# A fused adapter and mixture-of-experts kernel: tile 1 gathered early, gate/up of tile 1 ahead of down of tile 0, gathers four tiles ahead

## The reference

```python
base = jnp.einsum('bsi,oi->bso', x, W_base)
h = jnp.einsum('bsi,ji->bsj', x, Wt)
z = jnp.einsum('bsj,brj->bsr', h, Ab); l = jnp.einsum('bsr,bor->bso', z, Bb)
y = base + jnp.einsum('bso,po->bsp', l, Wp) * sc[:, None, None]
probs = jax.nn.softmax(y @ gate_w.T, axis=-1)
topk_w, topk_idx = jax.lax.top_k(probs, 2)            # then normalised to sum 1
g, u = (jnp.einsum('th,eih->tei', y, w) for w in (w_gate, w_up))
out = x + jnp.einsum('te,teh->th', combine, jnp.einsum('tei,ehi->teh', silu(g) * u, w_down))
```

## Time and profile before

| | |
|---|---|
| median of 3 runs | 370.98 us (370.84 to 372.6) |
| the profiled execution's own time | 370.85 us |
| its span in the trace | 369.0 us |
| PE busy | 351.7 us, 95% of the span |
| ACT, DVE, POOL busy | 179.0, 196.9, 135.3 us |

### The profile page before, as it was taken

How to read it: one execution, slowest core, us unless ns; L and a number is a source line. 1 busy time by engine, 2 the same in 40 slices (tenths; PEclk the granted TensorE clock), 3 DMA queues, 4 the chain that set the end, 5 groups by cost and what they waited for, 6 DMA issues and landing times.

```text
span 369.0 us, 7595 instructions
## 1 busy us (share of the span) xinstructions
PE 351.7 (95%) x2053; PEld 310.5 (84%) x2053; DVE 196.9 (53%) x272; ACT 179.0 (48%) x242; POOL 135.3 (37%) x85
## 2 busy tenths in 40 slices
PE   8999999998889999999999999999999999999980
PEld 4777788777789999999999999999999998898860
DVE  0566799782185445362854727548263556556210
ACT  2488611621464554645647356474555467454320
POOL 0000000024532525382753635546355455532131
PEclk9999999999999999999999999999999999999996
DMA  7994755873759676949297793956948575921322
GB/s 280 399 434 142 293 222 185 265 291 96 260 175 301 171 203 138 297 76 309 46 283 249 189 322 68 285 178 210 314 95 254 116 213 167 304 37 10 51 33 36
DMA packets 28914, 73.78 MB, mean 200 GB/s; under 512 B 3441, under 2 KB 3569, under 8 KB 28785
## 3 DMA queue, kind: packets, MB, share of 16 engines
q1 hardware_dynamic: 19904, 54.30, 41.9%
q0 software_dynamic: 8960, 18.89, 23.5%
HBM read 60.59 MB, written 19.92 MB: 218 GB/s over the span
## 4 chain that ended last, share of the span: by engine, by line
PE 80%; DMA 8%; issue 5%; DVE 2%; ACT 1%; POOL 1%; DVEq 1%; POOLq 1%; SPq 0%; ACTq 0%
PE bank L632 35%; PE bank L651 20%; PE bank L566 4%; PE bank L505 4%; PE bank L610 4%; PE bank L506 3%; PE bank L507 3%; PE bank L402 3%; DMA xg<-y_rows,gidx 3%; DMA w_raw<-wall 2%; DMA head_sb<-head 2%; PE bank L433 1%; DMA y_rows<-y_st 1%; PE bank L515 1%; POOL xg L1111 1%
## 5 line engine op out<-in xcount | busy, mean ns | idle before, releaser
L1128 POOL DMA_INDIRECT out<-ys,sidx x40 | 78.3, 1957 | 132.1 <-ACT ys L780 65.8
L1111 POOL DMA_INDIRECT xg<-y_rows,gidx x40 | 56.5, 1412 | 95.4 <-issue 84.2
L340 DVE TENSOR_TENSOR w_lo<-w_raw,w_hi (+2 forms) x32 | 76.3, 2383 | 19.9 <-ACT w_hi L338 14.3
L632 PE MATMUL bank<-w_hi,xt_hi 128*128 x320 | 80.7, 333 | 0.2 <-issue 0.2
L632 PE MATMUL bank<-w_hi,xt_lo 128*128 x320 | 77.1, 322 | 0.0
L632 PE MATMUL bank<-w_lo,xt_hi 128*128 x320 | 77.1, 322 | 0.0
L338 ACT ACTIVATE w_hi<-w_raw (+2 forms) x32 | 64.8, 2024 | 7.4 <-issue 4.9
L771 ACT ACTIVATE sg<-bank 128x352 f32<-128x352 f32 x40 | 18.6, 464 | 80.7 <-PE bank L632 79.9
L632 PEld LDWEIGHTS bank<-w_hi,xt_lo 128*128 128x128 f32 x320 | 55.8, 188 | 0.0
L632 PEld LDWEIGHTS bank<-w_lo,xt_hi 128*128 128x128 f32 x320 | 55.7, 188 | 0.0
L632 PEld LDWEIGHTS bank<-w_hi,xt_hi 128*128 128x128 f32 x320 | 53.9, 189 | 1.1 <-issue 1.0
(11 more groups left out here) (175 smaller groups left out, 370.3 us busy)
## 6 DMA issues: line engine op xcount, KB each, us to landing
w_raw<-wall SPq DMA_DIRECT2D x16, 1408.0 KB
w_raw<-wall SPq DMA_DIRECT2D x16, 768.0 KB, 10.6
x_st<-xt SPq DMA_DIRECT2D x8, 512.0 KB, 13.0
y_rows<-y_st SPq DMA_DIRECT2D x16, 256.0 KB, 4.5
head_sb<-head SPq DMA_DIRECT2D x2, 640.0 KB, 5.2
wb_sb<-wb SPq DMA_DIRECT2D x2, 512.0 KB, 8.9
wbt_sb<-wbt SPq DMA_DIRECT2D x2, 512.0 KB, 10.7
xg<-y_rows,gidx POOLq DMA_INDIRECT x40
```

The costliest lines, as they stand in the source:

```text
L340: e.tensor_tensor(w_lo[:, bass.ds(dst, n)], raw, hi, ALU.subtract).then_inc(own, 1)
L632: mm = e.matmul(bank[2 + 2 * s + t % 2][:, 0:INTER], a, w[:, bass.ds(at + (k * GU + s * INTER), INTER)], start=k == 0 and a is hi and w is ...
L1111: e.indirect_dma_start(out=xg[t % NXG][:], out_offset=None, in_=y_dram, in_offset=bass.IndirectOffsetOnAxis(ap=gidx[:, t:t + 1], axis=0)). ...
L1128: e.indirect_dma_start(out=out, out_offset=bass.IndirectOffsetOnAxis(ap=sidx[:, t:t + 1], axis=0), in_=ys[t % NYS][:], in_offset=None, bou ...
```

## The change

Tile 1 is gathered as soon as the stores that it needs have landed, as tile 0 is (`toks` and `need` have two columns in place of one, and POOL repeats its waits for t = 0 and 1). PE transposes tile 1 in the middle of `gate_up(0)`, does `gate_up(1)` ahead of `down(0)`, and the loops of PE, ACT and DVE begin at round 2. The token weights' matmuls write bank 7 in place of bank 5, and the three matmuls on zeros are gone. On ACT the high part of tile 3's gate and up weights stands ahead of `silu(1)`. POOL issues `gather(2)` and `gather(3)` after all stores, and then `gather(t+4)` ahead of `scatter(t)`. `N_LATE` stays 5, and SP's code is not changed.

```diff
-N_WARM0, N_WARM1 = 20, 3
+N_WARM0 = 20
-N_EARLY, C_FLOOR = 2, 12
+N_EARLY, C_FLOOR, N_AHEAD = 2, 12, 4
@@ PE
+                for i in range(N_EARLY):
+                    mm = e.matmul(bank[7][0:1, i * P:(i + 1) * P], toks[:, i:i + 1], ident, start=True, stop=True)
+                mm.then_inc(m_need, 1)
...
                     for k in range(KH):
+                        if t == 0 and k == KH // 2:
+                            x_turn(e, count, 1)
...
             gate_up(0)
             e.wait_ge(v_ohq, 1)
-            slot_tables(bank[5], 2, TABS)
+            e.wait_ge(v_need, 1)
+            slot_tables(bank[7], 2, TABS - 2)
             words[1] = tile_word(e, 1)
             h_turn(0)
-            x_turn(e, count, 1)
-            keep_warm(N_WARM1)
+            gate_up(1)
+            x_turn(e, count, 2)
+            words[2] = tile_word(e, 2)
             down(0)
             with ExitStack() as rest:
-                for t in range(1, NTILE + 1):
+                for t in range(2, NTILE + 1):
@@ ACT
             split_weights(e, count, 1, ahead, "gu", a_gu)
+            x_evac(1)
             silu(0)
             split_weights(e, count, 1, ahead, "dn", a_dn)
             h_evac(0)
-            x_evac(1)
-            ahead = tile_word(e, 2)
-            split_weights(e, count, 2, ahead, "gu", a_gu)
+            word = tile_word(e, 2)
+            split_weights(e, count, 2, word, "gu", a_gu)
+            ahead = tile_word(e, 3)
+            split_weights(e, count, 3, ahead, "gu", a_gu)
+            silu(1)
+            x_evac(2)
+            split_weights(e, count, 2, word, "dn", a_dn)
+            y_weighted(0)
@@ DVE
-            step(e.tensor_reduce(need[:], bank[7][0:1, P:2 * P], AX_X, ALU.max))
+            step(e.tensor_reduce(need[:], bank[7][0:1, 0:N_EARLY * P].rearrange("p (i n) -> p i n", n=P), AX_X, ALU.max))
@@ POOL
-            gather(0)
+            for t in range(N_EARLY):
+                top = table(e, T_REX, T_NEED + t, C_FLOOR * P - 1, NTOK - 1)
+                stores = [e.snap((top + P * (NYST - i)) // SEQ * 16) for i in range(NYST)]
+                for i in range(NYST):
+                    e.wait_ge(d_y[i], stores[i])
+                e.sem_inc(p_turn, 1)
+                gather(t)
             for i in range(NYST):
                 e.wait_ge(d_y[i], 16 * (CH // NYST))
-            for t in range(1, NXG - 1):
+            for t in range(N_EARLY, N_AHEAD):
                 gather(t)
...
-                    if t + NXG - 1 < NTILE:
-                        gather(t + NXG - 1)
+                    if t + N_AHEAD < NTILE:
+                        gather(t + N_AHEAD)
                     scatter(t)
```

More of the change, by code:

```diff
@@ L212, in build @@
         T_TILES, T_RUNS, T_NEED = NEXP, NEXP + 1, NEXP + 2
-        tok_0, need = r_c("tok_0", [P, 1], F32), r_c("need", [1, 1], F32)
+        toks = r_c("toks", [P, N_EARLY], F32)
+        need = r_c("need", [1, N_EARLY], F32)
         tabs = r_c("tabs", [1, NTAB, TQ], I32)
@@ L546, in need_turn, with slot_tables @@
                 e.wait_ge(v_tok, 1)
-                e.matmul(bank[7][0:1, P:2 * P], tok_0[:], ident, start=True, stop=True).then_inc(m_need, 1)
-            def slot_tables(dst, first, last):
+                for i in range(N_EARLY):
+                    mm = e.matmul(bank[7][0:1, i * P:(i + 1) * P], toks[:, i:i + 1], ident, start=True, stop=True)
+                mm.then_inc(m_need, 1)
+            def slot_tables(dst, first, n):
                 for j in range(NSEL):
-                    mm = e.matmul(dst[:, first * TQ:last * TQ], oh_m[:, j],
-                                  oh_q[:, j, first:last].rearrange("p a n -> p (a n)"),
+                    mm = e.matmul(dst[:, 0:n * TQ], oh_m[:, j],
+                                  oh_q[:, j, first:first + n].rearrange("p a n -> p (a n)"),
                                   start=j == 0, stop=j == NSEL - 1)
@@ L620, in gate_up @@
                         e.wait_ge(a_y, CH)
-                        e.wait_ge(v_w, 1)
                     e.wait_ge(v_xt, t + 1)
@@ L642, in down @@
                     e.wait_ge(v_dn, run + 1)
+                    if t == 1:
+                        e.wait_ge(v_w, 1)
                     if t >= 2:
@@ L794, in _ @@
                         ahead = tile_word(e, t + 2)
-                    if t == 1:
-                        y_weighted(0)
                     if 3 <= t <= NFULL:
@@ L1020, in _ @@
             e.tensor_tensor(gidx[:], tok_a[:], bank[4][:, TQ:2 * TQ], ALU.add).then_inc(v_gidx, 1)
-            e.tensor_tensor(tok_0[:], tok_a[:, 0:1], bank[4][:, TQ:TQ + 1], ALU.add).then_inc(v_tok, 1)
+            e.tensor_tensor(toks[:], tok_a[:, 0:N_EARLY], bank[4][:, TQ:TQ + N_EARLY], ALU.add).then_inc(v_tok, 1)
             step(e.tensor_scalar(emp_f[:], bank[4][:, 0:TQ], 1.0, float(SKIP), ALU.is_lt, ALU.mult))
@@ L1027, in _ @@
             e.wait_ge(m_need, 1)
-            step(e.tensor_reduce(need[:], bank[7][0:1, P:2 * P], AX_X, ALU.max))
-            e.tensor_scalar(tabs[:, T_REX, T_NEED:T_NEED + 1], need[:], float(C_FLOOR * P - 1), None, ALU.max).then_inc(v_need, 1)
+            step(e.tensor_reduce(need[:], bank[7][0:1, 0:N_EARLY * P].rearrange("p (i n) -> p i n", n=P), AX_X, ALU.max))
+            e.tensor_scalar(tabs[:, T_REX, T_NEED:T_NEED + N_EARLY], need[:], float(C_FLOOR * P - 1), None, ALU.max).then_inc(v_need, 1)
             e.wait_ge(v_w12, 1)
@@ L1069, in _ @@
             split_weights(e, count, 1, word, "gu", v_gu)
+            y_low(1)
             product(0)
             e.wait_ge(m_tb, 2)
-            step(e.tensor_copy(wtab[:], bank[5][:, 4 * TQ:5 * TQ]))
-            step(e.tensor_tensor(wtab[:], wtab[:], bank[5][:, 3 * TQ:4 * TQ], ALU.add))
-            e.tensor_tensor(wtab[:], wtab[:], bank[5][:, 2 * TQ:3 * TQ], ALU.add).then_inc(v_w, 1)
+            step(e.tensor_copy(wtab[:], bank[7][:, 2 * TQ:3 * TQ]))
+            step(e.tensor_tensor(wtab[:], wtab[:], bank[7][:, TQ:2 * TQ], ALU.add))
+            e.tensor_tensor(wtab[:], wtab[:], bank[7][:, 0:TQ], ALU.add).then_inc(v_w, 1)
             h_low(0)
-            y_low(1)
             split_weights(e, count, 1, word, "dn", v_dn)
+            word = tile_word(e, 2)
+            split_weights(e, count, 2, word, "gu", v_gu)
+            product(1)
+            y_low(2)
+            split_weights(e, count, 2, word, "dn", v_dn)
             with ExitStack() as rest:
-                for t in range(1, NTILE + 1):
+                for t in range(2, NTILE + 1):
                     go_on(e, rest, count, t - 1)
@@ L1084, in _ @@
                         h_low(t - 1)
-                    if t == 1 or NFULL <= t < NTILE - 1:
+                    if t == 2 or NFULL <= t < NTILE - 1:
                         split_weights(e, count, t + 1, word, "gu", v_gu)
+                    if t == 2:
+                        h_low(t - 1)
                     if t + 1 < NTILE:
                         y_low(t + 1)
-                    if t == 2:
-                        h_low(t - 1)
-                    if 2 <= t < NFULL:
+                    if 3 <= t < NFULL:
                         split_weights(e, count, t + 1, word, "gu", v_gu)
```

## The result

The changed kernel takes 381.96 us (median of 4 runs, 379.7 to 383.16) where the kernel before took 371.31 us beside it (4 runs, 370.84 to 372.6). The ratio is 1.0254, its 95% interval 1.0215 to 1.0292: about 2.5% slower, and outside the predicted range. The profiled execution was the fastest of the four, 379.70 us with a span of 377.9 us, which is 8.85 us more than the profiled execution of before.

A forecast was written before the change was run, and what follows sets the result against it. PE was taken as the bound (busy 192.00 of 192.00 us from 108 to 300 us). The 4.7 us won went to the stall, net +0.1; gathers +0.2 and median offset 0.13 on 370.85 gave 371.3 us, range 368.3 to 373.8.

The forecast's parts named there:

- the sum for that stall: Chain from down(0) through scatter(0), gather(5) and run 2's weights to h_turn(3): about 114.2 us, PE stalled 4.5 us.
- `ys(0)` done, with the row above in it: On ACT: down(0) ends at 96.2 us, ys takes 0.69 us more, so done at 96.9 us.
- `scatter(0)` on POOL: Length of scatter(0): 2.1 us, the middle of 1.61 to 2.60 us.
- its end to the weights' issue: gather(5) lands 2.36 us after it is made, then SP's registers take 0.55 us; weights issued at 104.1 us.
- weights to ACT: Run 2's gate and up weights, from SP's issue to ACT's release: 6.5 us, ending at 110.6 us.
- "ACT's long wait" rival: ACT's unresolved idle ahead of ys of tile 0 returns, holding it by 3 us: 374.3 us, chance 0.12.
- The clock: Rival: PE falls to half clock in the stall at h_turn(3), costing 1.5 us more: 372.8 us, chance 0.2.
- Gathers four ahead: Scatters lag around the weights of runs 4 and 5: 0.2 us added, from nothing to 1.5.
- The steps on PE's order: PE's reordered work at the turn: h_turn(3) possible at 109.7 us instead of 114.32, a win of 4.7 us.
- the step on tile 1's wait: PE's 1.66 us wait for gather(1) at the turn is gone, as its rows come early.
- `need`: DVE's reduction for two tiles plus PE's second small matmul delay gate_up(0) by 0.3 us, to 83.0 us.
- "Weights issued near 104 us": Sign to look for: SP issues run 2's weights near 104 us and not 97.

The follow-up runs named there:

- run 2: Not a follow-up run: part of the kernel's own work, whose weights tile 5 needs; SP issued them at 108.25 us in the changed kernel, 97.29 before.
- the low part moved back: Changed kernel with DVE's low part of tile 3's gate and up weights back behind its old neighbours, after scatter(0): 375.46 us, ratio 1.0085.
- the second trace of the change: The changed kernel unaltered, timed again beside the run with 84 matmuls on zeros: 379.05 us, ratio 1.0193.
- seven ahead: Changed kernel with gathers seven ahead in place of four: 367.19 us, ratio 0.9891.
- weights after `gather(4)`: Changed kernel, gathers still four ahead, with SP waiting for gather(4) in place of gather(5) before it issues run 2's weights: 370.61 us, ratio 0.9971.
- before with four ahead: The kernel before the change with gathers four ahead and nothing else of the change: 373.88 us, ratio 1.0047.
- 48 on zeros: Changed kernel with 48 matmuls on zeros ahead of h_turn(3), in PE's stall: 379.02 us, ratio 1.0188.
- five ahead: Changed kernel with gathers five ahead in place of four: 368.43 us, ratio 0.9918.
- late weights and seven ahead: Changed kernel with gathers seven ahead, SP waiting for gather(8), behind scatter(0), before run 2's weights: 379.82 us, ratio 1.021.
- 84 on zeros: Changed kernel with 84 matmuls on zeros ahead of h_turn(3): 378.08 us, ratio 1.0161.

## Why the prediction was wrong

The mechanism was named: the gain is given back at `h_turn(3)` to run 2's weights, because `gather(5)` passes behind `scatter(0)`. The step that failed is the sum for that stall. Its terms, as forecast and as the trace of after has them:

| term | forecast | measured | off by |
|---|---|---|---|
| `down(0)` ends | 96.2 | 96.00 | -0.2 |
| `ys(0)` done, with the row above in it | 96.9 | 97.09 + 0.69 = 97.78 | +0.9 |
| from there to `scatter(0)` | 0.9 | 98.67 - 97.78 = 0.89 | 0 |
| `scatter(0)` on POOL | 2.1 (to 2.6) | 4.47 | +2.4 |
| gap and `gather(5)` | 1.3 | 0.30 + 0.99 | 0 |
| its end to the weights' issue | 2.9 | 108.25 - 104.43 = 3.82 | +0.9 |
| weights to ACT | 6.5 | 115.32 - 108.25 = 7.07 | +0.6 |
| high part, `silu`, `hh` | 3.5 | 118.83 - 115.32 = 3.51 | 0 |
| `h_turn(3)` | 114.1 | 118.83 | +4.7 |

The first two rows and the last are points in time, the others lengths.

**The mis-sized term above all is the scatter.** The prediction took 2.1 us, the middle of 1.61 and 2.60 us. It placed both values "around DVE's weight work", but did not look at which of DVE's instructions ran beside the 2.60, nor where that one would stand after the change. The trace of before had the answer in two rows: the scatter of 2.60 us began at 108.09 and ended at 110.69 us, and DVE's timeline had the second of these rows in that time:

```profile
103.88 3.09 DVE L340 TENSOR_TENSOR w_lo<-w_raw,w_hi  x1 [0.23 <-issue]
...
107.48 1.76 DVE L340 TENSOR_TENSOR w_lo<-w_raw,w_hi  x1
```

That `w_lo` ended at 109.24, and the scatter 1.45 us later. After the change `w_lo` of tile 3 ends at 98.56 + 3.09 = 101.65 and `scatter(0)` at 103.14, 1.49 us later. A scatter that begins while a `w_lo` is running lasts until `w_lo`'s end plus its own 1.5 us or so. The change moved `w_lo` of tile 3 from 103.88 us, where no scatter was, to 98.56, which is 0.11 us ahead of `scatter(0)`. The run with the low part moved back shows it as cause: 1.61 us.

**The 0.9 us between the gather and the weights' issue are the gather's landing.** It was made on POOL at 104.43 us and landed at 103.44 + 4.25 = 107.69, 3.26 us later, where the prediction took 2.36 from `gather(1)`; SP's 108.25 - 107.69 = 0.56 us are as forecast. The chain of the changed kernel:

```profile
103.44 4.25 DMA xg<-y_rows,gidx
108.25 6.59 DMA w_raw<-wall
```

**The late `ys(0)` is the "ACT's long wait" rival in part.** `h_turn(0)` was over on PE at 89.11 + 0.49 = 89.60 us, but ACT began `ht_hi` at 92.01, with a releaser that the profile doesn't resolve. That pushed the high part of tile 3 to 93.82, `silu(1)` to 96.28 and `ys(0)` to 97.09. It also made the wait of 2.08 us at `x_turn(3)` that was not forecast. The rival was real, then, but it held `ys` of tile 0 by 0.9 us and not by 3.

**The clock** was a rival with a chance of 0.2; it should have been part of the sum. No row of before showed the 1.5 us of its price. The runs show more: from 118.90 to 123.30 us the granted clock was 0.51, which is (1 - 0.51) x 4.40 = 2.2 us of work lost, and 1.7 us between `x_turn(5)` and `x_turn(6)` in the second trace of the change. In 98 to 103 us it was 0.66 already, behind a wait of 2.08 us, worth (1 - 0.66) x 5.00 = 1.7 us, which the stall behind it swallowed, since `h_turn(3)` hung on the weights. The Trainium skill (TensorE: Matmul & The Clock Gate, "HAM oscillation — how this bites in real kernels") has a PE that waits for a DMA start its next burst at half clock; the trace agrees behind the stall of 5.57 us, and the prediction gave that too small a chance.

**Gathers four ahead** were priced at 0.2 us, up to 1.5: the trace shows a wait of 1.62 us at tile 10, and tiles 10 to 13 of the ledger lose 9.07 - 6.89 = 2.2 us. With early weights the price was 370.61 - 367.19 = 3.4 us, clock included.

The whole, by the ledger: `h_turn(3)` came at 118.83 us against 114.16 in the timeline of before, 4.7 us late, where the forecast had nothing; up to `x_turn(6)` the half clock adds 2.1; tiles 7 to 13 add 2.3, nearly all of it gathers, where the forecast had 0.2. That is the 9.07 us, and 8.85 at the end.

The steps on PE's order were right: 4.7 us forecast; with seven ahead PE was 4.18 us early though `x_turn(0)` came 0.55 us late there. So was the step on tile 1's wait, which is gone. `need` was put at 0.3 us. In the trace of after it cost nothing (`gate_up(0)` began at 82.67 against 82.71), but over the ten traces with the new order `x_turn(0)` began between 79.77 and 81.56 us against 80.19 before, so this term isn't settled. "Weights issued near 104 us" was right in kind and 4 us too early.

## What to carry to other kernels

Before an instruction is passed behind another in a queue, list every engine that waits for its semaphore: here one gather's place on POOL held up 2176 KB of weights that a different engine issues, and one more gather ahead turned a loss of 8 to 11 us into a gain of 3. When one duration of an operation has two values in a trace (1.61 and 2.60 us), find what runs beside each, and which of the two began first, before you take a middle. A stall of PE as long as the ones here (5.5 to 8.4 us) is priced with the half clock behind it, as part of the sum.

## What the runs showed of the hardware

**A running `w_lo` on DVE holds up an indirect DMA on POOL that begins after it, and not one that began before it.** `w_lo` is a subtraction of two fp32 tiles in SBUF, 3.09 us long for gate and up and 1.76 us for down. Worked out over the six traces of before, after, and the runs with weights after `gather(4)`, seven ahead, before with four ahead, and 48 on zeros:

| scatters | how many | length | end behind `w_lo`'s end |
|---|---|---|---|
| met no `w_lo` | 92 | 1.54 to 1.61 us | |
| began 0.04 us or more after a `w_lo` that was running | 88 | up to 4.50 us | 1.42 to 1.49 us (one 1.56) |
| `w_lo` began later, or at most 0.03 us sooner | 60 | 1.54 to 1.59 us | |

So it is not the overlap that costs: in the last row up to 1.57 us of overlap cost nothing, and those `w_lo` were no longer than others but for a few hundredths. Gathers do the same: 61 that began in a running `w_lo` ended 0.85 to 0.96 us behind its end, and those that met none took 0.94 to 0.99 us, but for the first of each kernel (2.5). The pair of rows in the run with five ahead (POOL, then DVE) shows it once more: `w_lo` began 0.13 us sooner, and the scatter's end is 1.48 us behind `w_lo`'s:

```profile
97.82 4.44 POOL L1145 DMA_INDIRECT out<-ys,sidx  x1 [4.85 <-ACT ys L788]
```

```profile
97.69 3.09 DVE L341 TENSOR_TENSOR w_lo<-w_raw,w_hi  x1 [0.63 <-issue]
```

The Trainium skill (SBUF — State Buffer, "Who interferes with whom") says that DVE and GpSimd share a pair of ports as an exclusive lock, so that the later one blocks. That fits the scatters which came later; a `w_lo` that came later was not held. The same section infers, though, that a `tensor_tensor` with both inputs in SBUF leaves descriptor generation alone. The runs contradict that for these indirect DMAs. Which of POOL's accesses is blocked is not shown.

**The clock can fall behind a short wait, but the length of the wait doesn't decide it.** It was low behind waits of 1.70 us (weights after `gather(4)`, 0.57), 2.00 us (low part later, 0.59 in 98.20 to 102.00 us), 2.08 us (after, 0.66) and 2.40 us (before with four ahead, 0.62); at the first the clock was still 1.00 in the 4 us up to the wait's end. Behind the 1.66 us of the earlier trace rows and the 1.62 us of after it stayed at 1.00, but so it did behind 1.87 us in the change's second trace and behind 2.77 us with late weights and seven ahead (timeline of PE, then the stretch behind the wait):

```profile
98.99 0.63 PE L569 MATMUL bank<-cs,xg 128*128 128x128 f32 x4 [2.77 <-DVE xt_lo L1064]
```

```profile
99.00:103.00 4.00, 4.00 (x27) 3.90 (x28) 3.53 (x3) 1.09 (x2) 3.42 (x1) 1.00 0.01 4
```

What decides is not shown.

**Left open:** why a result of PE reaches ACT and DVE late, once, at the turn (5.34 us of unresolved wait before, 4.26 after). It wasn't tried alone. The gathers back to back, which the prediction suspected, are no sufficient cause: with seven ahead they stood there in a row, and ACT began `ht_hi` at 90.18 us without such a wait. Nor is it shown why weights that are issued at 108 us land after 7 us in one execution and after over 8 us in the next. The six traces with late weights hint at `scatter(1)`: the sooner POOL was done with it behind the weights' issue, the later ACT had the weights.

| trace | POOL done with `scatter(1)`, after the weights' issue | ACT begins the high part, after the issue |
|---|---|---|
| low part later | 5.68 us | 6.87 us |
| after | 2.56 us | 7.07 us |
| seven ahead, late weights | 1.17 us | 8.28 us |
| 84 on zeros | 1.15 us | 8.25 us |
| the change once more | 0.93 us | 8.25 us |
| 48 on zeros | 0.41 us | 10.20 us |

No run moved `scatter(1)` by itself, so this is an order in six traces and not a cause shown.
